# Six message blocks before the first convolution, and a new order in the last group of a graph network layer

## The reference

```python
# x: (32, 256, 128), adj: (32, 256, 256)
h = relu(bn1(conv1d(x.T, w1x1)));  h = bn2(conv1d(h, w17, pad=8))
x_conv = relu(h + x.T).T
s = x @ w_se.T + b_se;  dist = |s_n|^2 + |s_m|^2 - 2 s_n.s_m
msg = relu(x @ w_msg.T + b_msg)
x_nmp = (exp(-dist) * adj) @ msg
y = gru([x_conv, x_nmp], x)          # gates r, z, n of width 128
x = layernorm(x + y)
h = (1 + eps) * x + adj @ x
x = layernorm(x + relu(h @ W1 + b1) @ W2 + b2)
```

## Time and profile before

| what | us |
|---|---|
| median of 3 runs | 400.33 (399.97 to 402.11) |
| the profiled execution, its own time | 399.86 |
| its span in the trace | 398.04 |
| PE busy | 378.2 (95%) |
| DVE, ACT, POOL busy | 281.0, 233.2, 231.3 |
| granted clock of TensorE, mean | 0.994 |

### The profile page before, as it was taken

The page is one execution under the profiler, slowest core; times in us unless marked ns, Lnnn a source line. Parts: engine busy times, 40 slices in busy tenths (PEclk is TensorE's granted clock), DMA queues, the critical chain, the costliest instruction groups (busy, mean ns, idle before and its releaser), DMA issues.

```text
span 398.0 us, 6585 instructions
## 1 busy us (share of the span) xinstructions
PE 378.2 (95%) x2329; PEld 336.2 (84%) x2329; DVE 281.0 (71%) x544; ACT 233.2 (59%) x424; POOL 231.3 (58%) x217
## 2 busy tenths in 40 slices
PE   2999999999999999999999999999999999999793
PEld 2889888998989989898888989899898998988673
DVE  4999878765885758865688558867587666865643
ACT  3663674467664665547844676637665378344934
POOL 4996357573494735665565734948347565654342
PEclk9999999999999999999999999999999999999989
DMA  7402000200120101301012011111012010000101
GB/s 244 199 2 106 2 24 31 105 28 26 55 77 30 54 2 53 107 1 53 0 53 105 6 46 53 62 44 54 0 54 106 0 55 2 1 2 0 53 2 53
DMA packets 7992, 19.39 MB, mean 49 GB/s; under 512 B 673, under 2 KB 5025, under 8 KB 6945
## 3 DMA queue, kind: packets, MB, share of 16 engines
q1 hardware_dynamic: 7536, 18.50, 13.3%
q10 hardware_dynamic: 432, 0.59, 0.4%
HBM read 14.89 MB, written 4.19 MB: 48 GB/s over the span
## 4 chain that ended last, share of the span: by engine, by line
PE 70%; DVE 12%; issue 6%; ACT 5%; POOL 4%; DMA 1%; DVEq 0%; ACTq 0%; SPq 0%; POOLq 0%
PE back L1117 29%; PE conv L1117 16%; PE front L1219 8%; PE back L1306 7%; PE conv L1171 4%; POOL rstd L497 4%; DVE xn L941 3%; PE front L1191 3%; DVE gbuf L905 1%; ACT tail L689 1%; DVE stats L919 1%; DVE usum L890 1%; DVE esum L884 1%; DVE hl L810 1%; DMA xv<-in_x_dram 1%
## 5 line engine op out<-in xcount | busy, mean ns | idle before, releaser
L1117 PE MATMUL conv<-sth,wh 128*128 128x256 f32 x280 | 84.7, 302 | 0.0
L1117 PE MATMUL conv<-sth,wl 128*128 128x256 f32 x280 | 79.9, 285 | 0.0
L1117 PE MATMUL conv<-stl,wh 128*128 128x256 f32 x280 | 79.9, 285 | 0.0
L497 POOL TENSOR_TENSOR rstd<-rstd,minus_half 128x4 f32<-128x4 f32 (+1 forms) x34 | 36.1, 1063 | 66.6 <-DVE rstd L923 66.6
L502 POOL TENSOR_TENSOR xw<-xw,xv 128x512 f32<-128x512 f32 (+1 forms) x17 | 20.9, 1228 | 59.8 <-ACT xw L673 59.8
L1117 PEld LDWEIGHTS conv<-sth,wh 128*128 128x128 f32 x280 | 52.9, 189 | 0.9
L1117 PEld LDWEIGHTS conv<-stl,wh 128*128 128x128 f32 x280 | 52.9, 189 | 0.9
L1117 PEld LDWEIGHTS conv<-sth,wl 128*128 128x128 f32 x280 | 52.9, 189 | 0.0
L515 POOL TENSOR_TENSOR amat<-amat,adjT 128x512 f32<-128x512 f32 x32 | 49.0, 1553 | 0.9
L1219 PE MATMUL front<-amat,msg 128*128 128x256 f32 x128 | 30.2, 379 | 0.0
L680 ACT ACTIVATE xch<-usum 128x512 fp32r<-128x512 f32 x16 | 10.1, 631 | 34.3 <-DVE usum L890 34.3
(11 more groups left out here) (216 smaller groups left out, 1020.6 us busy)
## 6 DMA issues: line engine op xcount, KB each, us to landing
adjT<-in_adj_dram SPq DMA_DIRECT2D x8, 1024.0 KB, 4.9
out_dram<-tail SPq DMA_DIRECT2D x15, 256.0 KB, 2.2
xv<-in_x_dram SPq DMA_DIRECT2D x7, 512.0 KB, 3.3
gbuf<-in_gates_dram SPq DMA_DIRECT2D x1, 576.0 KB, 6.4
tail<-in_conv_dram ACTq DMA_DIRECT2D x2, 256.0 KB, 3.9
xv<-in_x_dram SPq DMA_DIRECT2D x2, 256.0 KB, 4.6
later_w<-in_later_dram SPq DMA_DIRECT2D x1, 452.0 KB, 6.2
tail<-in_conv_dram SPq DMA_DIRECT2D x1, 320.0 KB, 5.2
```

The lines of the kernel that those rows point to most:

```text
L497: done(pool.tensor_tensor(rstd[:, k, h, q], rstd[:, k, h, q], minus_half[:, q], ALU.pow), RSTD[k])
L1117: ins = pe.matmul(bank, a, b, start=first and k == 0, stop=last and k == len(todo) - 1)
```

## The change

Weights: the message bias moves ahead in `later_w`, and the columns up to `W1_AT` (264 floats in each partition, 135 KB) become a transfer of their own with its own semaphore, issued behind x and ahead of the tap weights. PE runs message banks 0 and 1 (six blocks) ahead of conv1 and bank 2 behind it; DVE takes them ahead of `gbias` and the tap sums. POOL puts `first_diff(0)` and `diff_a(0)` ahead of L537. In every steady group three tap matmuls go ahead of `mlp1(gb, 0)`. In the last group ACT runs the gates of all three items before the `out_norm` of group 6; the aggregation of item 0 is cut in two, its first graph between two transposes; the output of the last item is normalised by DVE in place of ACT.

```diff
 # SP
+    LAST_READY = stage("last_out_ready", 0)
             def store(g, h, c=None):
-                wait(sp, OT_READY, g, item(h, c) + 1)
+                if (h, c) == LAST_ITEMS[-1]:
+                    wait(sp, LAST_READY, g, 1)
+                else:
+                    wait(sp, OT_READY, g, item(h, c) + 1)
...
                 done(sp.dma_start(xv[0][:, cols(1)], x_v[0, :, cols(1)]), X_LOADED)
+                sp.dma_start(later_w[:, 0:W1_AT], t["later"][:, 0:W1_AT]).then_inc(msg_w_loaded, 16)
                 sp.dma_start(c2raw[:, 0:5, :], t["conv2"][:, 0:5, :]).then_inc(conv2_loaded, 16)
                 sp.dma_start(c2raw[:, 5:9, :], t["conv2"][:, 5:9, :]).then_inc(conv2_loaded, 16)
-                sp.dma_start(later_w[:, :], t["later"]).then_inc(later_loaded, 16)
+                sp.dma_start(later_w[:, W1_AT:], t["later"][:, W1_AT:]).then_inc(later_loaded, 16)
 # POOL prologue
+                first_diff(0)
+                diff_a(0)
                 pool.wait_ge(conv2_loaded, 64)
                 pool.tensor_tensor(qsum[:, 5:9, :], ...).then_inc(tap_sums_ab, 1)
-                first_diff(0)
-                diff_a(0)
 # ACT last
-                gates(g, 0, WHOLE)
+                for h, c in LAST_ITEMS:
+                    gates(g, h, c)
                 out_norm(g - 1, 0)
-                gates(g, 1, 0)
+                h_high(g, 0, WHOLE)
                 out_norm(g - 1, 1)
-                gates(g, 1, 1)
-                for h, c in LAST_ITEMS:
-                    h_high(g, h, c)
+                h_high(g, 1, 0)
+                h_high(g, 1, 1)
                 for h, c in LAST_ITEMS:
                     hidden(g, h, c)
-                for h, c in LAST_ITEMS:
+                for h, c in LAST_ITEMS[:-1]:
                     out_norm(g, h, c)
 # DVE
+            def out_apply(g, h, c):
+                wait(dve, RSTD[1], g, item(h, c) + 1)
+                for q in part_blocks(c):
+                    last = dve.tensor_scalar(ot[:, h, q, :], ot[:, h, q, :], stats[:, 1, h, q, 1:2],
+                                             rstd[:, 1, h, q:q + 1], ALU.subtract, ALU.mult)
+                done(last, LAST_READY)
 # DVE prologue
                 x_low(0, 0, 1)
+                dve.wait_ge(msg_w_loaded, 16)
+                dve.wait_ge(factors_set, 2)
+                messages(0, 0)
+                messages(0, 1)
                 link(...)  # gbias, then the tap sums
...
+                messages(0, 2)
+                factors(0)
                 dve.wait_ge(later_loaded, 16)
-                dve.wait_ge(factors_set, 2)
-                for k in range(3):
-                    messages(0, k)
-                factors(0)
 # DVE last
                 out_stats(g, 1, 0)
+                out_shift(g, 0, WHOLE)
                 out_stats(g, 1, 1)
-                for h, c in LAST_ITEMS:
-                    out_shift(g, h, c)
+                out_shift(g, 1, 0)
+                out_apply(g, 1, 1)
 # PE prologue
+                pe.wait_ge(x_pair0_loaded, 16)
+                wait(pe, X_LOADED, 0, 16)
+                pe.wait_ge(msg_w_loaded, 16)
+                messages(0, 0, 0, 2)
                 pe.wait_ge(w_low, 1)
                 conv1(0, 0, 0)
                 conv1(0, 0, 1)
-                pe.wait_ge(later_loaded, 16)
-                messages(0, 0)
+                messages(0, 0, 2, 3)
 # PE steady
+                taps(gm, 7, 2, 3)
                 mlp1(gb, 0)
-                taps(gm, 7, 2, 3)
                 mlp1(gb, 1)
 # PE last
                 y_transpose(g, 1, 0)
+                aggregate(g, u, 0, WHOLE, (0,))
                 y_transpose(g, 1, 1)
-                for h, c in LAST_ITEMS:
-                    aggregate(g, u, h, c)
+                aggregate(g, u, 0, WHOLE, (1,))
+                aggregate(g, u, 1, 0)
+                aggregate(g, u, 1, 1)
```

More of the change, by code:

```diff
@@ L69, in laid_out @@
     o["later"] = np.concatenate([f["L0_gnn_w_msg"].T, f["L0_gnn_w_se"].T, np.zeros((P, 1), np.float32),
-                                 np.tile(f["L0_gnn_b_se"], (P, 1)), np.zeros((P, 1), np.float32), f["L1_gnn_W1"],
+                                 np.tile(f["L0_gnn_b_se"], (P, 1)), np.zeros((P, 1), np.float32),
+                                 np.tile(f["L0_gnn_b_msg"], (P, 1)), f["L1_gnn_W1"],
                                  f["L1_gnn_W2"].reshape(2, P, D).transpose(1, 0, 2).reshape(P, 2 * D),
-                                 np.tile(f["L0_gnn_b_msg"], (P, 1)), np.tile(f["L1_gnn_b2"], (P, 1))], axis=1)
+                                 np.tile(f["L1_gnn_b2"], (P, 1))], axis=1)
     o["consts"] = np.eye(P, dtype=np.float32)
@@ L100, in gnn_kernel @@
         c1raw = first_w[:, NVEC:NVEC + P]
-        W1_AT = MSGW + 4
+        BMSG_AT = MSGW + 4
+        W1_AT = BMSG_AT + P
         W2_AT = W1_AT + HID
-        later_w = sb("later_w", [P, W2_AT + 2 * D + 2 * P])
+        later_w = sb("later_w", [P, W2_AT + 2 * D + P])
         wmsg_se = later_w[:, 0:MSGW]
@@ L107, in gnn_kernel @@
         w2 = later_w[:, W2_AT:W2_AT + 2 * D].rearrange("p (f d) -> p f d", d=D)
-        bmsg = later_w[:, W2_AT + 2 * D:W2_AT + 2 * D + P]
-        b2bc = later_w[:, W2_AT + 2 * D + P:W2_AT + 2 * D + 2 * P]
+        bmsg = later_w[:, BMSG_AT:BMSG_AT + P]
+        b2bc = later_w[:, W2_AT + 2 * D:W2_AT + 2 * D + P]
         rs = sb("rs", [P, 2])
@@ L278, in gnn_kernel @@
         gates_loaded = sem("gates_loaded")
+        msg_w_loaded = sem("msg_w_loaded")
         later_loaded = sem("later_loaded")
@@ L1179, in conv1, with messages @@
                 done(products(conv1_bank(h, ahead)[:, :], [weights("conv1", 0) + (xh[u][:, cols(h)], xl[u][:, cols(h)])]), C1_FULL)
-            def messages(g, u):
-                wait(pe, XL_READY, g, 2)
-                for k, (q0, q1) in enumerate(MSG_BANKS):
+            def messages(g, u, k0=0, k1=3):
+                if k0 == 0 and k1 == 3:
+                    wait(pe, XL_READY, g, 2)
+                for k, (q0, q1) in list(enumerate(MSG_BANKS))[k0:k1]:
                     if k < 2:
@@ L1213, in distances, with gather @@
                 done(ins, DIST_FULL)
-            def gather(tile, c, lhs, rhs):
-                for k, b in enumerate((c,) if halved(c) else range(2)):
+            def gather(tile, c, lhs, rhs, graphs=(0, 1)):
+                for k, b in enumerate((c,)) if halved(c) else [(b, b) for b in graphs]:
                     for rm in range(PAR):
@@ L1271, in y_transpose, with aggregate @@
                 done(ins, Y_FULL)
-            def aggregate(g, u, h, c=None):
+            def aggregate(g, u, h, c=None, graphs=(0, 1)):
                 i = item(h, c)
@@ L1280, in aggregate @@
                 wait(pe, ADJE_READY, g, 2 * h + 2)
-                done(gather(bank("agg", h, c), c, lambda b, rm: xn[:, h, PAR * b + rm, :],
-                            lambda b, rm: adjT[u][:, 2 * h + b, rm, :]), AGG_FULL)
+                ins = gather(bank("agg", h, c), c, lambda b, rm: xn[:, h, PAR * b + rm, :],
+                             lambda b, rm: adjT[u][:, 2 * h + b, rm, :], graphs)
+                if graphs[-1] == 1:
+                    done(ins, AGG_FULL)
             def mlp1(g, h, c=None):
```

## The result

| | median us (range) | ratio to the kernel before |
|---|---|---|
| before, 6 runs | 400.44 (399.97 to 402.11) | |
| changed, 6 runs | 396.48 (396.18 to 396.81) | 0.9894, 95% interval 0.9873 to 0.9914 |

The change gains 4.0 us, 1.1%. The forecast was 394.5 with a range of 392.8 to 397.4: the sign and the range hold, the size is 2.0 us too large. The profiled execution took 396.81, its span is 395.0 (before 398.04) and its mean granted clock 0.999 (before 0.994). It is the slowest of its six.

A forecast was written before the change was run, and what follows sets the result against it. PE was taken as the bound, busy 95% of the span. Terms 1.0 - 2.5 - 2.9 - 1.2 = -5.6 against the profiled 399.86 gave 394.3, set at 394.5 us for the median; range 392.8 to 397.4.

The forecast's parts named there:

- the start: Start of the kernel: first_taps(0) waits for DVE's sums, now behind message work; a loss of 1.0 us.
- The working up to `first_taps(0)`: At the start: DVE's chain of tap sums lets first_taps(0) start at 13.1, where before it was 12.10.
- PE's start: First matmul: PE starts when the new transfer lands, taken as 6.85, which is 0.3 earlier.
- so this is covered too, by 2 to 3 us: Start: POOL's masks end at about 32.5, PE needs the last two at 35 or later, so no loss.
- the last group: Last group: earlier gates, records in PE's gap and the clock staying at 2.4 GHz; a gain of 2.9 us.
- The port race: Rival, at the start: DVE loses the shared port to POOL; loss 2.9 in place of 1.0, 396.4 us; chance 0.18.
- the steady groups: Seven steady groups: three tap matmuls fill PE's wait for h_low, 0.36 us each; a gain of 2.5 us.
- the gates: Last group: ACT's gates ahead of out_norm make item 2's t2 1.35 us earlier; 1.3 of the 2.9 gain.
- the end: End: item 0's shift earlier and DVE normalising item 2 bring the last store forward; a gain of 1.2 us.
- The rivals of the clock: Last group: the clock still falls or xn holds the aggregation; 1.5 us less gain, 396.0 us; chance 0.12.
- of the steady groups: Rival: in steady groups h_low comes later by what PE is earlier, so no gain; 397.0 us; chance 0.06.
- of the ReLUs: Rival, steady groups: mlp2(gb, 0) waits for ACT's second ReLU, cover 0.5 us; slower than before; chance 0.03.

The follow-up runs named there:

- e1: The changed kernel with the start of before on all engines; 393.83 us, ratio 0.9841 to the kernel before.
- e2: The kernel before with the new start alone; 403.23 us, ratio 1.0074.
- e3: The kernel before with the new tap order in the steady groups alone; 397.93 us, ratio 0.9937.
- e8: e1 with item 0's aggregation in one piece behind the last transpose; 394.32 us, ratio 0.9848 to the kernel before.
- e12: e1 with ACT's output norms back between the gates and item 0's aggregation in one piece; 396.94 us, ratio 0.9912 to the kernel before.
- e11: e1 with ACT's output norms of group 6 back between the last group's gates; 395.97 us, ratio 0.9878 to the kernel before.
- e7: The changed kernel with DVE's and POOL's lists at the start as before; 395.17 us, ratio 0.9863 to the kernel before.
- e5: The changed kernel with DVE's list at the start as before; 396.55 us, ratio 0.9895 to the kernel before.
- e10: The changed kernel with PE, DVE and POOL in the old order at the start, separate transfer kept; 394.39 us, ratio 0.9837 to the kernel before.
- e6: The changed kernel with POOL's list at the start as before; 395.66 us, ratio 0.9869 to the kernel before.

## Why the prediction was right and wrong

**Wrong: the start, +1.0 predicted, +3.3 in the profiles and +2.1 to +3.0 in the times.** The working up to `first_taps(0)` was right in its structure: it said 6.25 after PE's start (13.1 less 6.85), and 13.91 less 7.52 is 6.39. PE's start was off, by 0.67: I took the new transfer to land at 6.85 by its size, and it landed at 7.38, as late as the larger tap slice had in that place; in the six profiles with this transfer it landed between 6.99 and 8.50. With 0.14 more of the working, that is 0.8 of the 2.3 us by which the start was mis-sized.

The other 1.5 come from a step that failed: "so this is covered too, by 2 to 3 us". I asked of each of DVE's and POOL's results when PE needs it next, found cover for the factors and the masks, and closed the sum. The cover was there: PE waited for neither. What I put at nothing is what POOL's later masks do to DVE, which was busy in 4.83 to 5.00 of each 5 us from 20 to 45 before, as the windows show (columns as in the earlier trace rows, busy by engine in the order PE, PEld, DVE, ACT, POOL):

```profile
25.00:30.00 5.00, 5.00 (x25) 4.25 (x24) 5.00 (x4) 3.07 (x6) 4.82 (x4) 1.00 0.00 0
```

DVE's operations get longer beside POOL: the two `usum` took 2.93 before, 3.43 in the changed kernel, and 1.28 in e1, where both ran behind the masks. DVE then came to the second group too late, and PE waited 0.8 for `esum` and 0.3 for `gbuf`.

Two figures of the working don't stand as given. The 0.22 for a message record is not in the earlier trace rows, where 16 records take 2.26 (0.14 each); it was right for the changed kernel all the same (twelve in 2.62). And two sums don't close: 2.9 for the lost race is less than its parts 1.0, 1.1 and 1.2, and the 4.9 for the last group in the range is more than its upper bounds 2.9 and 1.5.

**The port race** was the rival that came nearest in time (396.4), and not what happened: the quads took 0.68 in the changed kernel. The time that it gave was near the measured one by another cause, and that the range held is luck in so far. The race did happen in e2 and e3, where `first_taps(0)` waited 1.52 and 2.36. Later, beside the masks, DVE's additions met POOL's too, and that is the part that cost.

**Right: the steady groups**, 2.5 predicted, 2.4 in the profiles, 2.5 by e3. The ReLUs kept their cover; no wait of `mlp2` appeared.

**Right: the last group**, 2.9 up to `mlp1` predicted, 2.93 measured; the gates 1.35, measured 1.30. The clock stayed up, as I took it to. The split of that gain was loose: I gave the clock and the records in the gap to the split aggregation, and e8 shows that the earlier gates alone would have kept the clock.

**Nearly right: the end**, 1.2 predicted, 1.0 measured.

The sum closes: -5.6, and 2.3 more at the start, 0.1 in the groups and 0.2 at the end, is -3.0, the difference of the spans. The rivals of the clock, of the steady groups and of the ReLUs fell; the start was the one term whose upper bound, 2.9, rested on the wrong mechanism.

## What to carry to other kernels

When a step is moved ahead of others, ask not only when its consumers need their results, but also which engine's work will now run beside which. Here POOL's masks were in time for PE and still cost it 1.5 us, because DVE ran longer beside them and had no room left until PE met it. A busy share of 71% over the whole span hid that: from 20 to 45 us DVE was busy nearly throughout. And look at both ends of a wait before moving what ends it: DVE's sums ended the wait before `first_taps(0)`, but `h1` was only 0.27 ahead of them. Lastly, before putting work into an idle gap of PE, look whether another edit already shortens the gap: two cures for one slow stretch don't add.

## What the runs showed of the hardware that was not expected

- A wait of 3.85 us brought the granted clock to 0.50 behind it in the profiles of the kernel before, e3 and e12 (e2: 3.8 and 0.50). Waits of 2.53 (e8) and of 2.95 with 0.76 soon after (e11) left it at 1.00. The Trainium skill ("TensorE: Matmul & The Clock Gate", Part 1) says that idle time halves the clock; the trace agrees for the long wait, and the shorter ones did not do it here.
- DVE operations on 80 columns took 1.30 and 1.27 us beside a busy POOL (0.24 and 0.20 alone), longer than an addition on 512 columns (0.68). Beside POOL in the kernel before they took 0.72 and 0.76, in e7 1.31 and 0.19. So next to POOL the cost of a small operation depends on which POOL instruction it meets, more than on its size.
- The new transfer (132 KB as the profile counts) landed 5.3 us after its issue, one of 320 KB issued at the same time before 5.2: the smaller one was not sooner. In the same place it took 4.9 (e2), 5.1 (e5, e7), 6.0 (e10) and 6.4 (e6), so its landing is not known to better than a microsecond or so.
